# Cross-attention and expert feed-forward on one core: outputs kept whole instead of in two halves of the columns

## The reference, cut to what matters

```python
x = x + xattn(layernorm(x), ctx_2048, ...)
h = rmsnorm(layernorm(x))                      # 2048 rows of 512
topv, topi = top_k(softmax(h @ router_w), 2)   # two experts a row
w_dense = zeros((t, e)).at[arange(t)[:, None], topi].set(topv / sum(topv))
g, u = einsum('td,edf->tef', h, w_gate), einsum('td,edf->tef', h, w_up)
eo = einsum('tef,efd->ted', silu(g) * u, w_down)
moe = einsum('te,ted->td', w_dense, eo)
sh = silu(h @ sw_gate) * (h @ sw_up) @ sw_down
x = x + moe + sh
```

## Time and profile before

| | |
|---|---|
| median of 3 runs | 826.72 us (823.37 to 827.68) |
| profiled execution, its own time | 826.63 us |
| its span, first to last instruction | 824.8 us |
| mean granted clock of TensorE | 0.993 |
| PE busy | 779.6 us (95%) |
| POOL busy | 364.5 us (44%) |
| scatters of line 1376 | 78, busy 123.1 us |
| gathers of line 1359 | 39, busy 39.6 us |

### The profile page before, as it was taken

How to read it: one execution, slowest core, us unless ns; L and a number is a source line. 1 busy time by engine, 2 the same in 40 slices (tenths; PEclk the granted TensorE clock), 3 DMA queues, 4 the chain that set the end, 5 groups by cost and what they waited for, 6 DMA issues and landing times. The chain is left out here.

```text
span 824.8 us, 11865 instructions
## 1 busy us (share of the span) xinstructions
PE 779.6 (95%) x3879; PEld 393.6 (48%) x3879; DVE 547.7 (66%) x1048; ACT 419.8 (51%) x800; POOL 364.5 (44%) x309
## 2 busy tenths in 40 slices
PE   7999999989999999999999999998999999999993
PEld 3433334334334343343343455775546666666662
DVE  6687898898888888888888767587653223223231
ACT  2124667767768777687776674310343333333331
POOL 4154227417429246173222421000138777777774
PEclk9999999999999999999999999999999999999998
DMA  8959275567565765666543235510946665666553
GB/s 290 216 148 198 62 164 139 115 131 153 126 150 125 157 154 125 132 149 154 116 99 122 94 105 196 238 52 25 340 119 103 94 98 97 102 99 99 90 96 45
DMA packets 54186, 109.67 MB, mean 133 GB/s; under 512 B 12200, under 2 KB 27304, under 8 KB 49888
## 3 DMA queue, kind: packets, MB, share of 16 engines
q1 hardware_dynamic: 37080, 79.39, 38.5%
q0 software_dynamic: 16960, 29.37, 18.8%
q10 hardware_dynamic: 88, 0.16, 0.1%
HBM read 67.90 MB, written 40.86 MB: 132 GB/s over the span
## 5 line engine op out<-in xcount | busy, mean ns | idle before, releaser
L1090 DVE TENSOR_REDUCE negmax<-front_ps 128x1 f32<-128x512 f32 x512 | 326.9, 684 | 68.6 <-PE front_ps L932 67.4
L824 ACT ACTIVATE probs<-st_ps 128x512 f32<-128x512 f32 x512 | 284.0, 598 | 139.4 <-PE st_ps L968 139.1
L1376 POOL DMA_INDIRECT out<-ring,row_i x78 | 123.1, 1578 | 62.5 <-ACT ring L1432 46.4
L1607 PE MATMUL big_ps<-w_gu,attn 128*128 x244 | 111.3, 593 | 0.8 <-ACT attn L1425 0.8
L656 POOL CAST early<-early 128x512 fp32r<-128x512 f32 x28 | 17.1, 612 | 162.3 <-ACT early L772 158.1
L968 PE MATMUL st_ps<-stacks 50*128 50x512 f32 x256 | 68.5, 493 | 2.2 <-ACT probs L824 2.0
L1359 POOL DMA_INDIRECT ring<-h_rows,row_i x39 | 39.6, 1016 | 68.7 <-DMA out<-x_sb 57.1
L1446 ACT ACTIVATE attn<-big_ps 128x256 f32<-128x256 f32 x39 | 15.0, 384 | 106.1 <-PE big_ps L1607 106.1
L1816 DVE TENSOR_TENSOR zeros<-attn,big_ps 128x256 f32<-128x256 f32 x39 | 16.4, 421 | 78.6 <-ACT attn L1446 78.6
L981 PE MATMUL pv_ps<-probs,v_t 128*32 128x512 f32 x512 | 68.2, 605 | 0.5 <-ACT probs L824 0.5
L981 PE MATMUL pv_ps<-probs,early 128*32 128x512 f32 x512 | 68.2, 605 | 0.3 <-ACT probs L824 0.3
(11 more groups left out here) (218 smaller groups left out, 1218.4 us busy)
## 6 DMA issues: line engine op xcount, KB each, us to landing
parts_dram<-early SPq DMA_DIRECT2D x32, 512.0 KB, 3.9
stacks<-parts_dram SPq DMA_DIRECT2D x32, 256.0 KB, 5.4
w_gu<-in_gate_up SPq DMA_DIRECT2D x8, 1024.0 KB, 12.2
x_sb<-in_x SPq DMA_DIRECT2D x8, 512.0 KB, 12.2
early<-in_ctx POOLq DMA_DIRECT2D x8, 512.0 KB, 5.7
stacks<-parts_dram SPq DMA_DIRECT2D x32, 128.0 KB, 5.7
k_stack<-parts_dram SPq DMA_DIRECT2D x16, 256.0 KB, 5.0
q_stack<-parts_dram SPq DMA_DIRECT2D x16, 256.0 KB, 5.6
```

Source lines behind the costliest of these rows:

```text
L824: nc.scalar.activation(probs[:, k % 2, u % GH, :], score_bank(UNITS * s + u), ACT.Exp, scale=SCALE).then_inc(exp_done, 1)
L1090: nc.vector.tensor_reduce(negmax[:, n % 2, c:c + 1], smax_bank(UNITS * n + u), AX_X, ALU.max, negate=True).then_inc(max_done, 1)
L1376: nc.gpsimd.indirect_dma_start(outs[i], bass.IndirectOffsetOnAxis(ap=row_i[:, k:k + 1], axis=0), y_sb[:, k % RING, DY * i:DY * (i + 1)], N ...
L1607: mm = nc.tensor.matmul(gu_ps[:, :], h_t[:, k % 2, a, :], w_gu[:, bass.ds(expert, 1), a, :], start=(a == 0), stop=(a == DT - 1))
```

## The change

The number of column pieces of the output goes from two to one:

```diff
-YCUT = 2
+YCUT = 1
 DY = D // YCUT
```

## The result

The changed kernel takes **839.87 us** (median of 4 runs, 838.48 to 841.72), the kernel before, timed beside it, 827.2 us (823.37 to 828.49). The ratio is 1.017, 95% interval 1.015 to 1.020: slower by 1.7%. Forecast were 823.3 us and a range up to 829.0. The first rival, the chain of whole scatters, has come true.

What follows compares the result with a forecast made beforehand. PE was taken to bound the blocks at 5.33 us each, with POOL nearly full and late gathers stalling PE; -2.5 us of stalls and -0.8 us at the end gave -3.3 us, so 823.3 us, range 820.5 to 829.0.

Steps and rivals of the forecast that it cites:

- The first rival: Blocks: each whole scatter waits for the last one's landing, which sets the pace; up to 838.6 us; chance 0.15.
- The stalls of PE: Blocks: gathers issued 1.85 us earlier on POOL end all five PE stalls from late gathers, -2.5 us.
- Issuing: POOL in the blocks: a whole scatter takes as long to issue as a half, 1.55 us.
- The second rival: Whole scatter cut again, or POOL's time follows the bytes: issuing 3.1 us, time 882 us; chance 0.04.
- The scatter's own transfer: Second half adds d = 0.76 us to one transfer (bounds 0.49 and 1.2); landing 4.53 us after the start.
- The 172 GB/s: DMA engines' rate in a half scatter once going, taken as peak rate for the second half's 131 KB: 0.76 us.
- The wait between scatters: Blocks: cycle from scatter to scatter grows from 4.52 to 5.28 us, still within PE's 5.33, costing nothing.
- The end: Last blocks: two issues become one, the data takes longer; last scatter starts at 813.47 us; -0.8 us.
- The closing 3.5: End of the span: 3.5 us from the last scatter's landing to the span's end, as in the kernel before.
- SP and the dump rows: 16 base stores go from SP (7 us), one 0.55 us clearing issue from POOL during attention: gain nothing.

Runs made afterwards that it cites:

- gather-first halves: Kernel before, two halves kept, but POOL issues the gather of block k + 4 ahead of the wait for block k's copy: 824.45 us, ratio 0.9980.
- The swapped waits: Changed kernel, but POOL waits first for the landing of the scatter before, then for ACT's copy: 828.24 us, ratio 1.0034.

## Why the prediction was wrong, point by point

**The stalls of PE.** Right as a reading of the kernel before: the gather-first halves recover them to a tenth of a us (176.0 us for blocks 5 to 38). Whole scatters in two chains recover them too (176.01 us). In the changed kernel the slower pace of the scatters hides any such gain.

**Issuing.** Right: the means are 1.59 us for a whole scatter and 1.58 for a half, and the medians lie between 1.55 and 1.58 us from 128 to 512 columns. The second rival falls.

**The scatter's own transfer: the step that failed.** "I take the peak rate [...] since the slow start of a transfer is paid once." The added half costs d = 5.65 - 4.52 = 1.13 us in the cycle, not 0.76; nearly all of it is the landing, 4.86 us on average in that chain against 3.77. So the cycle is above PE's 5.33 us and not 0.05 below. The 172 GB/s were the pace of one quarter of a microsecond in one half, not the pace at which more bytes are moved. Whole transfers from their first byte to their last (columns as the earlier trace rows), a half before:

```profile
815.00:816.25 1.25, 0.00 (x0) 0.00 (x0) 0.00 (x0) 0.00 (x0) 0.62 (x1) 1.00 0.94 104
```

and two whole scatters of the changed kernel:

```profile
821.00:823.50 2.50, 0.00 (x0) 0.00 (x0) 0.00 (x0) 0.00 (x0) 0.00 (x0) 0.79 0.94 105
826.75:829.25 2.50, 0.00 (x0) 0.00 (x0) 0.00 (x0) 0.00 (x0) 0.00 (x0) 0.50 0.83 105
```

Twice the bytes take twice the time, at the same mean pace (the half of the earlier trace rows was slower still, 87 GB/s over 1.5 us). Nor is a slow start paid once. The first half microsecond of a half's transfer before, beside its later pace:

```profile
813.00:813.50 0.50, 0.00 (x0) 0.00 (x0) 0.00 (x0) 0.00 (x0) 0.50 (x1) 1.00 0.88 45
813.75:814.25 0.50, 0.00 (x0) 0.00 (x0) 0.00 (x0) 0.00 (x0) 0.50 (x1) 1.00 0.98 156
```

and of the first of the two whole scatters:

```profile
821.00:822.00 1.00, 0.00 (x0) 0.00 (x0) 0.00 (x0) 0.00 (x0) 0.00 (x0) 1.00 1.15 45
822.50:823.25 0.75, 0.00 (x0) 0.00 (x0) 0.00 (x0) 0.00 (x0) 0.00 (x0) 0.50 1.03 188
```

Here 45 GB/s last 0.5 us for the half and 1.0 us for the whole one. The first microsecond of the second whole scatter runs at 94 GB/s, though, so the slow phase has no fixed shape, and what makes it stays open. The prediction's own upper bound, the busy time of a half once more (1.2 us), was nearest. The estimated price of 0.30 us for the second half (the Trainium skill, "DMA: Bandwidth & Descriptors", "Anatomy of one DMA — SWDGE (gpsimd) path") is further off: the fit of the Trainium skill has 436 GB/s, and these scatters, which add, grow by some 0.5 us for each 64 KB, about 125 GB/s.

**The wait between scatters.** The mechanism, its place and the point from which it decides (d = 0.81) stood in the first rival, with a chance of 0.15, and its formula 790.0 + 39d gives 834.1 us for d = 1.13. The span is 836.6: the chain began 1.0 us earlier, and the drain adds 3.55. The swapped waits show what the 0.75 us in that cycle were worth: with scatters as wide, landing after the same 4.9 us, 11.6 of the 12.7 us come back. What was wrong is the weight. A cover of 0.05 us under a d known only between 0.49 and 1.2 is none: about half of that interval lay beyond 0.81. The 0.75 us "seen once" turned out to be there in every cycle.

**The end.** The last scatter was to start at 813.47 us and started at 824.76, all of it the chain. "The closing 3.5" was carried over as a constant; it became 7.0 us, so this term was 3.5 us short, whatever d is. No row of before told that, since it shows one drain only.

**SP and the dump rows.** Right: with whole stores and half scatters there is no difference (ratio 1.0003).

## What to carry to other kernels

Merging two transfers that form separate chains of waits makes one chain with a longer link; what decides is not the issues saved but landing plus restart against the pace of the busiest engine, and that sum has to be taken at its upper bound when the cover is a few per cent. Where two waits stand ahead of a DMA, the order matters: put the one that is met last first, so that the restart it causes is the short one (0.27 us instead of 0.75 here). If an engine is late because a prefetch stands behind other issues, move the prefetch; here that took the 2.5 us of stalls out of the blocks, as the merge was hoped to, though the median fell by only 0.2%.

## What the runs showed of the hardware that was not expected

- Where two waits are written ahead of an indirect DMA, the second stands alone on POOL's queue, and about 0.75 us pass from it to the start of the DMA; after the other wait it can be 0.27 us. The order of two source lines made 11.6 us. Why the two differ is not shown.
- A scatter that adds lands some 0.5 us later for each 128 fp32 columns of its 128 rows, from 128 to 512 columns; over its whole transfer it runs at about 104 GB/s, as a half or as a whole. Issuing takes 1.55 to 1.58 us at any of these widths.
- The drain of POOL at the end lasted between 2.4 and 6.8 us, changing with the transfers that POOL had issued in the program, but not with their number alone.
